# First attention with stacked single-pass scores, and expert weight buffers given up earlier

## The reference

```python
for L in range(4):
    x = x + graph_L(layernorm(x), adj)
    x = x + experts_L(layernorm(x))
# graph_0
neib_att = tanh(neigh @ Wn1 + bn1) @ Wn2 + bn2          # 1024 x 32
x_att    = tanh(x @ Wx1 + bx1) @ Wx2 + bx2              # 1024 x 32
ws = x_att @ neib_att.T + einsum('nkh,nh->nk', tanh(edge_emb[adj] @ We + be), x_att)
ws = softmax(where(adj > 0, leaky_relu(ws, 0.01), -9e15), axis=1)
out = concat([x @ Wfx + bfx, ws @ value + ...])
# experts_L: top 2 of 16, 8, 8, 16 experts, inner width 512, 512, 1024, 512
y = sum over the chosen experts e of weight_e * (act(x @ w1[e] + b1[e]) @ w2[e] + b2[e])
```

## Time and profile before

| | us |
|---|---|
| three runs | 1258.81, 1261.8, 1266.55 |
| profiled execution | 1265.98 |
| its span | 1264.0 |
| TensorE busy in it | 964.2 |
| mean granted TensorE clock | 0.863 |

### The profile page before, as it was taken

The page is one execution under the profiler, slowest core; times in us unless marked ns, Lnnn a source line. Parts: engine busy times, 40 slices in busy tenths (PEclk is TensorE's granted clock), DMA queues, the critical chain, the costliest instruction groups (busy, mean ns, idle before and its releaser), DMA issues. The chain is left out here.

```text
span 1264.0 us, 22113 instructions
## 1 busy us (share of the span) xinstructions
PE 964.2 (76%) x7102; PEld 875.1 (69%) x7102; DVE 740.7 (59%) x1712; ACT 511.2 (40%) x941; POOL 452.2 (36%) x572
## 2 busy tenths in 40 slices
PE   5786389808688738955973999999928995499993
PEld 1555288804677738854873899999914884499993
DVE  4435567664688655657434566666553674566664
ACT  2032067600366516642101777777603551243441
POOL 1031246410599514630000255555303440244431
PEclk9677599957799958987995899999958996699997
DMA  6001296520000015743112654653240001544764
GB/s 217 1 1 35 88 316 221 166 85 7 1 1 1 2 56 186 254 158 104 55 30 96 263 199 166 235 196 128 76 129 1 1 1 35 219 155 160 249 238 160
DMA packets 65605, 148.31 MB, mean 117 GB/s; under 512 B 10464, under 2 KB 42496, under 8 KB 59520
## 3 DMA queue, kind: packets, MB, share of 16 engines
q1 hardware_dynamic: 55552, 120.17, 27.7%
q0 software_dynamic: 9984, 27.28, 6.4%
HBM read 203.88 MB, written 18.87 MB: 176 GB/s over the span
## 5 line engine op out<-in xcount | busy, mean ns | idle before, releaser
L1345 PE MATMUL r_pH<-e_xsT,e_w 128*128 128x128 f32 x2624 | 319.4, 280 | 13.8 <-DMA e_w<-w_in 9.7
L1345 PEld LDWEIGHTS r_pH<-e_xsT,e_w 128*128 128x128 f32 x2624 | 308.1, 196 | 20.1 <-issue 12.9
L1293 POOL DMA_INDIRECT y_rows<-e_ys,e_to x104 | 179.3, 1724 | 264.3 <-DVE e_idx L1413 145.3
L1381 ACT ACTIVATE e_w_hi<-e_w 128x1024 fp32r<-128x1024 f32 (+1 forms) x104 | 136.4, 1312 | 128.8 <-DMA e_b<-b_in 95.0
L1425 DVE TENSOR_TENSOR e_w_lo<-e_w,e_w_hi 128x1024 fp32r<-128x1024 f32 (+1 forms) x104 | 161.0, 1548 | 40.7 <-ACT e_w_hi L1381 28.5
L1358 PE MATMUL r_pY<-e_w_hi,e_h_hi 128*128 128x256 f32 x544 | 163.0, 300 | 10.1 <-issue 8.2
L1430 DVE TENSOR_TENSOR e_h_lo<-xnT,e_h_hi 128x512 fp32r<-128x512 f32 (+1 forms) x104 | 89.1, 857 | 124.4 <-ACT e_h_hi L1397 118.3
L1358 PE MATMUL r_pY<-e_w_hi,e_h_lo 128*128 128x256 f32 x544 | 154.5, 284 | 0.0
L1358 PE MATMUL r_pY<-e_w_lo,e_h_hi 128*128 128x256 f32 x544 | 154.5, 284 | 0.0
L346 PE MATMUL g_o<-g_V,g_pT 128*128 128x65 f32 (+2 forms) x896 | 139.2, 310 | 15.3 <-ACT g_pT L306 15.2
L346 PEld LDWEIGHTS g_o<-g_V,g_pT 128*128 128x128 f32 x896 | 124.2, 195 | 31.4 <-issue 21.2
(11 more groups left out here) (247 smaller groups left out, 1396.1 us busy)
## 6 DMA issues: line engine op xcount, KB each, us to landing
e_w<-w_in SPq DMA_DIRECT2D x60, 1024.0 KB
e_w<-w_in SPq DMA_DIRECT2D x72, 512.0 KB
e_w<-w_in SPq DMA_DIRECT2D x32, 1028.0 KB
e_w<-w_in SPq DMA_DIRECT2D x44, 514.0 KB
e_b<-b_in SPq DMA_DIRECT2D x76, 128.0 KB
e_w<-y_rows SPq DMA_DIRECT2D x24, 256.0 KB, 5.1
p_adj<-adj_in SPq DMA_DIRECT2D x8, 512.0 KB, 7.0
xn_rows<-xn SPq DMA_DIRECT2D x4, 1024.0 KB, 4.4
```

Source lines behind the costliest of these rows:

```text
L1293: pool.indirect_dma_start(out=y_rows[:, :], in_=ys[b][:, :], in_offset=None, out_offset=bass.IndirectOffsetOnAxis(ap=to[b][:, :], axis=0))\
L1345: ins = nc.tensor.matmul(pH[b % 2][:, f, :], w1[b][:, at:at + P], xsT[b % 2][:, c, :], start=(c == 0), stop=(c == DC - 1))
L1381: nc.scalar.activation(w2_hi[b % 2][:, :], w2[b][:, :], ACT.Copy).then_inc(w2_rounded, 1)
```

## The change

In the first graph part `xa` and `na` become 96-partition tiles in float32r. Their three bands of 32 partitions hold, for `xa`, the rounded value, the rest and the rounded value, and for `na` the rounded value, the rounded value and the rest. One matmul over 96 partitions so sums rounded x rounded, rest x rounded and rounded x rest in one pass. To fill the bands the second projection uses weights repeated three times, ScalarE writes all bands with the bias, and VectorE then replaces one band by the rest. Five more small bias loads stand behind the loads of `adj`. `S` gets two tiles and `tp` one (`deep`), and the scores run two units ahead.

In the expert parts the load of `w1` waits for the activations of tile t-4 (`h_ready`; in layer 3 `h_summed`), that of `w2` for `w2_split` of tile t-4, and `b2` has a semaphore and a step of its own, two tiles behind.

```diff
-            tp = [ph.ps(f"tp{n}", [P, NT, P]) for n in range(2)]
+            deep = 1 if scores else 2
+            tp = [ph.ps(f"tp{n}", [P, NT, P]) for n in range(deep)]
...
                 def turn(u):
                     pe.wait_ge(shifted, u + 1)
                     for hf in range(2):
-                        if u >= 2:
-                            pe.wait_ge(exped, 2 * (u - 2) + hf + 1)
+                        if u >= deep:
+                            pe.wait_ge(exped, 2 * (u - deep) + hf + 1)
...
                 if scores:
-                    scores(0).then_inc(scored, 1)
+                    for u in range(2):
+                        scores(u).then_inc(scored, 1)
                 for u in range(units + 3):
+                    if scores and u + 2 < units:
+                        pe.wait_ge(maxed, u + 1)
+                        scores(u + 2).then_inc(scored, 1)
                     if 2 <= u < units + 2:
                         turn(u - 2)
-                    if scores and u + 1 < units:
-                        pe.wait_ge(maxed, u + 1)
-                        scores(u + 1).then_inc(scored, 1)
...
-                xa = ph.sb("xa", [HID, N])
-                na = ph.sb("na", [HID, N])
+                xa = ph.sb("xa", [3 * HID, N], F32R)
+                na = ph.sb("na", [3 * HID, N], F32R)
+                X_LO, N_LO = slice(HID, 2 * HID), slice(2 * HID, 3 * HID)
...
+                        for dst, src in again:
+                            sp.dma_start(dst, src).then_inc(again_loaded, 16)
...
+                        act.wait_ge(again_loaded, 16 * len(again))
+                        for n, (t, ps) in enumerate(((xa, psA), (na, psB))):
+                            act.wait_ge(mm, 3 + n)
+                            nc.scalar.activation(t[:, :].rearrange("p (a b) -> p a b", a=2), ps[0:3 * HID, :, :],
+                                                 ACT.Identity, bias=cols[:, 2 * n + 1:2 * n + 2]).then_inc(rounded, 1)
...
+                        nc.vector.tensor_copy(wx2r[:, :, :], bc(wx2[:, :].unsqueeze(1), [HID, 3, HID]))
...
-                            dve.wait_ge(mm, 3 + n)
-                            nc.vector.tensor_scalar(t[:, :].rearrange("p (a b) -> p a b", a=2), ps[0:HID, :, :],
-                                                    cols[:, 2 * n + 1:2 * n + 2], None, ALU.add).then_inc(copied, 1)
+                            dve.wait_ge(rounded, n + 1)
+                            halves = t[lo, :].rearrange("p (a b) -> p a b", a=2)
+                            nc.vector.scalar_tensor_tensor(out=halves, in0=ps[lo, :, :],
+                                                           scalar=cols[lo, 2 * n + 1:2 * n + 2],
+                                                           in1=halves.bitcast(F32), op0=ALU.add,
+                                                           op1=ALU.subtract).then_inc(copied, 1)
...
-                S = ph.ps("S", [P, 2, 512])
+                S = [ph.ps(f"S{n}", [P, 2, 512]) for n in range(2)]
...
                         if not early(i, b, UN):
-                            sp.wait_ge(y_ready, t - UN + 1)
+                            sp.wait_ge(h_summed if kind == "silu" else h_ready, t - UN + 1)
+                            sp.nop(nofuse=True)
...
+                        if not early(i, b, UN):
+                            sp.wait_ge(w2_split, t - UN + 1)
+                            sp.nop(nofuse=True)
...
-                        if b2_name:
-                            sp.dma_start(b2[b][:, :], A[b2_name][bass.ds(e, 1), :].to_broadcast([P, D]), **other)\
-                                .then_inc(w2_loaded[b], 16)
+                        if b2_name and not early(i, b, 2):
+                            bias(*before(i, b, 2))
...
+                    def bias(i, b):
+                        t = UN * i + b
...
+                            sp.wait_ge(y_ready, t - UN + 1)
...
+                        sp.dma_start(b2[b][:, :], A[b2_name][bass.ds(e, 1), :].to_broadcast([P, D]), **other)\
+                            .then_inc(b2_loaded[b], 16)
...
-                        act.wait_ge(w2_loaded[b], W2_INC * (i + 1))
+                        act.wait_ge(w2_loaded[b], 16 * (i + 1))
...
                         if b2_name:
+                            dve.wait_ge(b2_loaded[b], 16 * (i + 1))
```

More of the change, by code:

```diff
@@ L430, in _ @@
                             ins.then_inc(mm, 1)
-                        for n, (w, src, ps) in enumerate(((wx2, tx, psA), (wn2, tn, psB))):
+                        pe.wait_ge(repeated, 1)
+                        for n, (w, src, ps) in enumerate(((wx2r, tx, psA), (wn2r, tn, psB))):
                             pe.wait_ge(tanhed, n + 1)
                             for hf in range(2):
-                                ins = nc.tensor.matmul(ps[0:HID, hf, :], w[:, :], src[:, hf * 512:(hf + 1) * 512],
+                                ins = nc.tensor.matmul(ps[0:3 * HID, hf, :], w[:, :, :], src[:, hf * 512:(hf + 1) * 512],
                                                        start=True, stop=True)
@@ L437, in _ @@
                         pe.wait_ge(copied, 2)
-                        nc.tensor.matmul(psA[0:HID, 0, 0:2], we[:, :], emb[:, :], start=True, stop=True)\
+                        nc.tensor.matmul(psA[0:2 * HID, 0, 0:2], wer[:, :, :], emb[:, :], start=True, stop=True)\
                             .then_inc(mm, 1)
@@ L538, in vector_end @@
                             op0=ALU.mult, op1=ALU.add)
-                attention(block, ph, 1, 0.01, lambda u: False, lambda u: S[:, :, :].rearrange("p a b -> p (a b)"),
+                attention(block, ph, 1, 0.01, lambda u: False, lambda u: S[u % 2][:, :, :].rearrange("p a b -> p (a b)"),
                           s, sa, lambda u, c: V[:, c, :], OUT + 1, finish, scores, {"vector_end": vector_end})
@@ L1228, in experts @@
                 w2_loaded = [ph.sem(f"w2_loaded{n}") for n in range(UN)]
+                b2_loaded = [ph.sem(f"b2_loaded{n}") for n in range(UN)]
                 y_stored = [ph.sem(f"y_stored{n}") for n in range(UN)]
@@ L1236, in experts @@
                 w1_v, w2_v = A[w1_name], A[w2_name]
-                W2_INC = 32 if b2_name else 16
                 def loop(eng, step):
@@ L1272, in step @@
                             .then_inc(w1_loaded[b], 16)
+                        if not early(i, b, UN):
+                            sp.wait_ge(w2_split, t - UN + 1)
+                            sp.nop(nofuse=True)
                         sp.dma_start(w2[b][:, :], w2_v[bass.ds(e, 1), :, :].rearrange("a p c -> (a p) c"), **other)\
                             .then_inc(w2_loaded[b], 16)
-                        if b2_name:
-                            sp.dma_start(b2[b][:, :], A[b2_name][bass.ds(e, 1), :].to_broadcast([P, D]), **other)\
-                                .then_inc(w2_loaded[b], 16)
+                        if b2_name and not early(i, b, 2):
+                            bias(*before(i, b, 2))
                         if early(i, b, 1):
                             sp.wait_ge(xs_loaded[0], 16)
+                    def bias(i, b):
+                        t = UN * i + b
+                        e = sp.value_load(etab[0:1, bass.ds(t, 1)], min_val=0, max_val=EN - 1)
+                        other = {}
+                        if not early(i, b, UN):
+                            sp.wait_ge(y_ready, t - UN + 1)
+                            sp.nop(nofuse=True)
+                            held = sp.value_load(etab[0:1, bass.ds(t - UN, 1)], min_val=0, max_val=EN - 1)
+                            other = {"cond": e != held}
+                        sp.dma_start(b2[b][:, :], A[b2_name][bass.ds(e, 1), :].to_broadcast([P, D]), **other)\
+                            .then_inc(b2_loaded[b], 16)
                     gate_load(sp)
-                    loop(sp, step)
+                    last = loop(sp, step)
+                    if b2_name:
+                        bias(last, UN - 2)
+                        bias(last, UN - 1)
                     sp.wait_ge(last_stored, 16 * UN)
```

31 lines of the change are left out of this document (20 added, 11 removed).

## The result

| | before | changed |
|---|---|---|
| runs, median us (lowest to highest) | 1263.0 (1258.8 to 1266.6), 6 runs | 1249.4 (1248.6 to 1254.5), 6 runs |
| profiled execution: span us, mean clock | 1264.0 | 1247.0, 0.861 |

The ratio is 0.990, with a 95% interval of 0.987 to 0.993. The change makes the kernel faster by 13.6 us. Forecast were 33.7 us less, so the time lies above the range (1217 to 1243). The ratio stands on the 1% that the prediction took as the least that a measurement can tell from no change. TensorE's busy time is 947.4 us where it was 964.2: most of the gain of 17 us in the span is time in which TensorE was busy.

The account below looks back on a forecast made before the run. It took the attention as bound by a mask-to-scores loop between VectorE and TensorE, the experts by TensorE when weights are on time. Attention -20.5, prologue +1.8, experts -15 sum to -33.7 us: 1228 us, range 1217 to 1243.

Parts of the forecast that it names:

- the new wait in `end`: Expert parts: VectorE's wait for the bias row, put at 0, with the row asked for 6.9 us ahead of need.
- the prediction's own signs of being wrong: Half-clock units past the first four, first products waiting for weights as long as now, or VectorE idle for bias rows.
- Its mechanism: Expert parts: `w1` asked for 3.4 to 5 us earlier, `w2` by about as much, so late loads come on time; -15 us.
- the prediction's best case of 22: Expert parts: far end of the term, nearly all of the lost 7.8 + 9.7 + 6.9 + 1.4 us regained.
- The slower rival: Expert parts: bias rows land late and `end` stops the line; 35 fresh rows, at 2 us each 1298 us; chance 0.03.
- weights that come no sooner: Expert parts: asking earlier only lengthens the queue, giving -4 instead of -15, so 1239 us; chance 0.11.
- the undecoupled scores: First attention: the single `tp` keeps units near 5.7 us, only low-clock units gain, some 5 us; 1244 us; chance 0.05.
- the best case of the prediction: First attention: masks at VectorE's own pace, then TensorE's, 33.9 us in all, 25 saved.
- The model: First attention paced like the second graph part: 0.6 + 24.8 + 13.4 = 38.8 us against 59.3, so 20.5 saved.
- the rival of a clock that stays low: First attention: TensorE stays at the low clock and binds, saving 6.5 instead of 20.5; 1242 us; chance 0.11.
- The rule on shared ports: First attention: a mask reading PSUM would not block GpSimd, the shift would; weighed, but the term stayed at -20.5.
- The prologue: Before the first attention: an added ScalarE step, +1.1 us, and late bias loads, perhaps 1; taken as +1.8, from +1.1 to +3.5.

Follow-up runs that it names:

- e11: The changed kernel, with SyncE taking the two experts of the bias row's tile from kept registers instead of loading them again; 1221.2 us, 0.967 of the kernel before.
- e9: The changed kernel with the bias row in its own tile's step, `w2` and bias behind `y_ready` of four tiles ago, only `w1` early; 0.972 of the kernel before.
- e10: The changed attention with the releases of before for all three expert buffers, and the bias row on its own semaphore; 0.980 of the kernel before.
- e5: The changed kernel, with the bias row of tile t-2 issued ahead of `w1` and `w2` of tile t instead of behind them; 0.993 of the kernel before.
- e3: The kernel before, with an unused second pair of value loads and a nop added to SyncE's step in layers with a bias; 1282.8 us, 1.013.

## Why the prediction was wrong, by its own steps

**The experts: the step that failed.** The prediction put the new wait in `end` at nothing and said that "SyncE's two added no-operations per tile lie in its waits". It counted the nops, and not the second pair of expert loads that `bias` issues. That pair is the dearest thing added: the 1.9 us gap against 0.6. I looked only for when each load is allowed to be issued, never for whether SyncE has the time to issue it. The timeline of before could have told: its `w1` issues in late layer 0 are 2.8 us apart at the closest, and 3.69 in the rows above, beside a tile of 3.43. An estimate from these, made after the fact: with 1.3 us more the step is 4.1 to 5.0 us, longer than a tile at either end, so late layer 0 takes 15 x 4.1 to 15 x 5.0 = 62 to 75 us. The trace says 68.95. Two of the prediction's own signs of being wrong came true: first products that wait for weights (19.8 us, more than before) and a VectorE idle for bias rows.

**Its mechanism held.** With the pair of loads gone and the rest of the change as it is (e11), late layer 0 gives 7.0 us of 7.8 (forecast 6), layer 1 7.3 of 9.7 (forecast 6), early layer 0 4.4 (forecast 1: the DMA engines' share of 0.96 was not a wall, they moved 378 GB/s there), and layer 3 2.3 (forecast 1.5). That is 21 us, near the prediction's best case of 22, and 43 us less than before in the whole kernel. e9 and e10 show which part does it: `w1`. In the changed kernel the layers lost 9.7 + 5.0 - 3.1 - 2.3 = 9.3 us instead of gaining 15.

**The clock made it dearer.** A late load costs idle time first. But in late layer 0 TensorE is also busy for 58.47 us, where e11 needs 51.98 for the same tiles. The first products behind two stalls of the changed kernel, and an undisturbed one:

```profile
171.88 3.10 PE L1387 MATMUL r_pH<-e_xsT,e_w 128*128 128x128 f32 x16 [2.48 <-DMA e_w<-w_in]
...
180.71 1.95 PE L1387 MATMUL r_pH<-e_xsT,e_w 128*128 128x128 f32 x16
...
187.76 3.75 PE L1387 MATMUL r_pH<-e_xsT,e_w 128*128 128x128 f32 x16 [3.45 <-DMA e_w<-w_in]
```

The windows of the two slow ones, with the granted clock as the third number from the end:

```profile
171.88:174.98 3.10, 3.10 (x17) 3.10 (x18) 1.28 (x4) 1.06 (x1) 0.37 (x2) 0.62 0.95 306
...
187.76:191.50 3.74, 3.74 (x17) 3.74 (x18) 1.95 (x4) 1.06 (x1) 0.77 (x1) 0.50 0.87 305
```

Over the whole stretch it is 0.90. Of the 16.7 us that separate the two kernels there, 6.5 are more busy time of TensorE and 10.2 are idle time. The slower clock accounts for about 6.1 of the 6.5: the tiles that begin at 171.88, 187.76 and 222.99, each behind a stall of 2.5 to 3.5 us, took 5.29, 5.99 and 5.10 us without idle time where 3.43 is undisturbed.

**The slower rival** was that the bias rows land late. They do (27.4 us of waits in 19 places), by its own count of 35 fresh rows under the 1.0 us from which it decides. But e5 took that wait away and gained nothing, so it was a right observation with a wrong mechanism. The rivals of weights that come no sooner (1239) and of the undecoupled scores (1244) lie nearer to the time than the forecast, and both are wrong in their reason.

**The attention.** Forecast -20.5, measured -25.5 in the window, half a us past the best case of the prediction; the window of 33.8 us is shorter than the 37 to 41 that it wanted to see. About 3 of these 5 us are a miscount. The model took 24.8 us from the first to the eighth mask of the second graph part, but the mask at 347.66 in the earlier trace rows is the ninth. The masks begin at 322.82, 323.97, 325.12, 329.76, 332.10, 337.66, 341.92 and 344.65, and the eighth is this one of the kernel before:

```profile
344.65 1.22 DVE L241 CUSTOM_DVE_ANT_0 g_g<-g_dst,neg 128x1024 f32<-128x1024 f32 x1
```

So the model's own start-up is 21.8 us and its term -23.5. In the first attention after the change it is 71.85 - 53.02 = 18.8, 3.0 less, and the steady pace is 3.1 us:

```profile
53.02 1.23 DVE L242 CUSTOM_DVE_ANT_0 g_g<-g_S,neg 128x1024 f32<-128x1024 f32 x1 [1.13 <-PE g_S L542]
...
68.71 1.21 DVE L242 CUSTOM_DVE_ANT_0 g_g<-g_S,neg 128x1024 f32<-128x1024 f32 x1
...
71.85 1.21 DVE L242 CUSTOM_DVE_ANT_0 g_g<-g_S,neg 128x1024 f32<-128x1024 f32 x1
```

The tail from the eighth mask on took 86.08 - 71.85 = 14.2 us instead of 13.4. One turn in it waited 0.99 us for an exponential at 78.19, where the prediction costed the single `tp` at nothing.

After the first, no mask waits for scores. The price of the scores was about right. At the high clock a pair keeps TensorE for 68.51 - 67.96 = 0.55 us, until its transposes begin (forecast 0.5), and at the low clock for 61.13 - 60.05 = 1.08 us (forecast 1.0). The two matmuls start 0.31 us apart, not 0.24. A record lasts longer than that, since it overlaps the next:

```profile
67.96 0.72 PE L542 MATMUL g_S<-g_na,g_xa 96*128 96x512 f32 x2
68.51 1.04 PE L337 MATMUL g_tp<-ident,g_lm 128*128 128x128 f32 x8
```

The mean clock of the window rose from 0.77 to 0.90, so the rival of a clock that stays low did not come.

**The rule on shared ports** holds where the prediction weighed it. Beside a mask, which reads `S` from PSUM, GpSimd's small instructions are short; beside the shift, both of whose large inputs are in SBUF, one takes nearly as long as the shift:

```profile
68.88 0.19 POOL L286 TENSOR_TENSOR g_small<-g_s,g_small 128x1 f32<-128x1 f32 x1
...
69.85 1.28 DVE L250 SCALAR_TENSOR_TENSOR g_lm<-g_g,g_small,g_t 128x1024 f32<-128x1024 f32 x1
70.01 1.17 POOL L281 TENSOR_TENSOR g_small<-g_small,g_s 128x1 f32<-128x1 f32 x1 [0.80 <-DVE g_small L242]
```

The Trainium skill, page "SBUF — State Buffer", section "SBUF: two separate sides", names a VectorE instruction with two SBUF inputs as one that takes the shared pair of ports for its whole length, and the trace agrees. What it gave shows at the start. In the second graph part GpSimd's first two instructions, beside masks with both inputs in SBUF, took 1.11 and 1.10 us, and the fourth mask came 4.64 us after the third: between them stands a shift, which waits for ScalarE and that for GpSimd. Here they took 0.19 and 0.26 us, and it came 58.30 - 55.31 = 2.99 us after. That is 1.65 of the 3.0 us; the rest was not traced. The steady 3.1 us is TensorE's own work: from 64.82 to 74.06 it has no idle time.

**The prologue.** Forecast +1.8; the window begins 52.28 - 49.90 = 2.4 us later. The guess that ScalarE would meet the bias columns late was right, at 1.8 us instead of 1:

```profile
30.42 1.11 ACT L488 ACTIVATE g_xa<-p_psA,p_cols 96x1024 fp32r<-96x1024 f32 x1 [1.82 <-DMA p_cols<-L_gnn_be_in]
```

**A sum by the right terms.** Attention -25.5, prologue +2.4, experts +9.3: -13.8 us. The terms are from the two profiled executions, whose spans differ by 17.0: between the stages 3 us more went, 2 of them between layers 0 and 1, that I didn't follow. That the sum falls on the -13.6 of the medians is luck.

## What to carry to other kernels

An engine that only issues transfers has a pace of its own. Where loads are conditional or indexed, read its shortest step from the timeline of its issues and put it beside the tile time of the engine that it feeds, before anything is added to the step. The page doesn't show it: such instructions don't count as busy, and a SyncE that is late shows up as other engines' waits for DMA. And the one wait that is new in a profile can be a second sign of the same lateness; an experiment that removes it alone is the cheap test.

## What the runs showed of the hardware

- A load of one value from SBUF into a SyncE register took 0.27 us, and a pair of them with their register operations added 1.0 to 1.3 us to a step: 1.90 us from `w2` to the bias against 0.87 with the pair replaced by moves (e11), and 0.62 before. Spent on a bound queue this was 16 us in e3 for 64 pairs. The Trainium skill, page "DMA: Bandwidth & Descriptors", section "Issuing engines are not separate DMA queues", says that issuing from several engines saves only the sequencer's time to start a DMA, "which is usually small relative to the DMA itself". The record of one issue is small here too, 0.33 us. It is the lookups around it that are not: a step of three conditional loads (1.18 MB) took 4.7 us on SyncE, while their transfer is an estimated 3.7 us at the 320 GB/s of the earlier trace rows, and some of these steps transfer nothing at all.
- A skipped conditional DMA still has its issue record (0.07 to 0.09 us instead of 0.33) and its lookups: in the changed kernel a step that skipped all its loads took 4.28 us (from 200.12 to 204.40) beside the 4.63 of one that made all three.
- TensorE's granted clock fell behind stalls of 2.48, 3.45 and 2.50 us in late layer 0 of the changed kernel, and stayed at 1.00 behind one of 1.98 us in layer 0 before. But the length of the last stall does not decide alone: in layer 1 of the changed kernel the clock was 0.81 behind a stall of 1.90 us, which came after three of 1.4 to 1.6 us in the 20 us ahead of it.
